# Retention in a six-stage Trainium2 kernel: rotation split by queries and keys, squares per head on ScalarE, layer norm on undivided numerators, and the output product in three one-pass products

## The reference

```
xn    = layernorm(x)
qkvg  = xn @ w_attn                       # 1024 q, 512 k, 512 v, 8 gates
log_g = log_sigmoid(6.906768 + gates)     # decay per token and key head
q, k  = rope(q), rope(k)
s     = q . k / 8
a     = exp(2*log(|s| + 1e-30) + cumsum(log_g)[t] - cumsum(log_g)[s] - max), 0 above the diagonal
num   = a @ v ;  den = sum(a)
y     = num / (den + 1e-6)
y     = (y - mean(y)) / sqrt(var(y) + 1e-9) * ln_w     # per head, 64 wide
x     = x + y @ w_proj                    # 1024 -> 512
```

## Time and profile before

| | |
|---|---|
| median of three runs | 2318.66 us |
| the profiled execution, its own time | 2317.28 us |
| its span, first to last instruction | 2315.5 us |
| TensorE busy | 2114.3 us, 91% |
| VectorE busy | 1419.9 us, 61% |
| ScalarE busy | 1362.7 us, 59% |
| GpSimd busy | 299.8 us, 13% |
| mean granted TensorE clock | 0.964 of full |
| retention stage | from 695 to 882 us of the span |

### The profile page before, as it was taken

How to read it: one execution, slowest core, us unless ns; L and a number is a source line. 1 busy time by engine, 2 the same in 40 slices (tenths; PEclk the granted TensorE clock), 3 DMA queues, 4 the chain that set the end, 5 groups by cost and what they waited for, 6 DMA issues and landing times. The chain is left out here.

```text
span 2315.5 us, 37828 instructions
## 1 busy us (share of the span) xinstructions
PE 2114.3 (91%) x14761; PEld 1633.6 (71%) x14761; DVE 1419.9 (61%) x2392; ACT 1362.7 (59%) x2595; POOL 299.8 (13%) x270
## 2 busy tenths in 40 slices
PE   6999999999968977799999979999999999866798
PEld 4777777777744545688888746877787777645676
DVE  5455555454544864499999854554554454667687
ACT  2566566566544433488888725666666665541675
POOL 2111112121110000100000221121111120101001
PEclk9999999999988988999999989999999999977999
DMA  4000010101004003599999730010100100022887
GB/s 155 19 23 35 20 38 20 38 19 38 1 1 179 1 1 130 223 386 367 356 358 364 268 141 19 20 38 19 38 20 19 38 20 19 2 73 105 325 336 265
DMA packets 53585, 262.34 MB, mean 113 GB/s; under 512 B 9496, under 2 KB 9880, under 8 KB 26528
## 3 DMA queue, kind: packets, MB, share of 16 engines
q1 hardware_dynamic: 47104, 244.71, 28.2%
q0 software_dynamic: 2560, 8.39, 1.1%
q10 hardware_dynamic: 3744, 6.82, 0.8%
HBM read 243.91 MB, written 15.99 MB: 112 GB/s over the span
## 5 line engine op out<-in xcount | busy, mean ns | idle before, releaser
L512 DVE COPY c_pt<-bank 128x512 f32<-128x512 f32 x256 | 177.0, 691 | 549.3 <-PE bank L341 549.2
L664 ACT ACTIVATE c_pr<-wide,c_nmax 128x512 f32<-128x512 f32 x512 | 349.3, 697 | 164.8 <-DVE c_nmax L504 83.8
L231 POOL TENSOR_TENSOR c_clo<-c_raw,c_chi 128x512 fp32r<-128x512 f32 x122 | 158.2, 1299 | 1012.1 <-ACT c_chi L641 1012.1
L341 PE MATMUL bank<-ident,c_pr 128*128 128x128 f32 x2048 | 268.7, 273 | 14.0 <-DVE c_pt L512 11.8
L341 PEld LDWEIGHTS bank<-ident,c_pr 128*128 128x128 f32 x2048 | 238.0, 140 | 49.9 <-DVE c_pt L512 14.0
L649 ACT ACTIVATE c_khi<-bank,c_cols 128x512 fp32r<-128x512 f32 x128 | 88.1, 688 | 252.2 <-PE bank L94 252.2
L92 PE MATMUL bank<-c_wv_hi,c_chi 128*128 128x512 f32 x512 | 218.2, 426 | 15.7 <-DVE c_clo L442 14.4
L1664 DVE TENSOR_TENSOR moe_wlo<-moe_raw,moe_whi 128x2048 fp32r<-128x2048 f32 x97 | 219.1, 2284 | 17.2 <-ACT moe_whi L1520 17.2
L92 PE MATMUL bank<-c_chi,c_wk_hi 128*128 128x512 f32 x512 | 213.7, 417 | 8.8 <-ACT c_v L655 8.7
L94 PE MATMUL bank<-c_wv_hi,c_clo 128*128 128x512 f32 x512 | 202.8, 396 | 0.0
L93 PE MATMUL bank<-c_wv_lo,c_chi 128*128 128x512 f32 x512 | 202.7, 396 | 0.0
(11 more groups left out here) (371 smaller groups left out, 4044.4 us busy)
## 6 DMA issues: line engine op xcount, KB each, us to landing
moe_hr<-in_L_ffn_w SPq DMA_DIRECT2D x68, 1024.0 KB, 7.0
moe_raw<-in_L_ffn_w SPq DMA_DIRECT2D x52, 1024.0 KB, 7.0
c_raw<-in_ctx SPq DMA_DIRECT2D x32, 1024.0 KB, 4.9
moe_raw<-in_L_ffn_we_gate SPq DMA_DIRECT2D x15, 1024.0 KB, 7.0
moe_raw<-in_L_ffn_we_up SPq DMA_DIRECT2D x15, 1024.0 KB, 6.6
moe_raw<-in_L_ffn_we_down SPq DMA_DIRECT2D x15, 1024.0 KB, 6.6
slot_outputs<-moe_ob ACTq DMA_DIRECT2D x26, 256.0 KB, 6.0
ret_w<-in_L_attn_w_attn SPq DMA_DIRECT2D x4, 1024.0 KB, 9.2
```

Source lines behind the costliest of these rows:

```text
L231: nc.gpsimd.tensor_tensor(clo[:, g % 2, c, :], raw[:, c, :], f32(chi[:, g % 2, c, :]), ALU.subtract) \
L341: last = pe.transpose(TB[n % 2][:, h * P:(h + 1) * P], pr[:, u % 2, h, n * P:(n + 1) * P], k["ident"][:])
L512: nc.vector.tensor_copy(pt[:, n, :], TB[0][:]).then_inc(pt_dve, 1)
L664: nc.scalar.activation(pr[:, u % 2, h, :], S[h][:], ACT.Exp, bias=nmax[:, b % 2, i, at:at + 1], scale=-1.0 if masked else 1.0, accum_out=d ...
```

## The change

- `rotate` is cut in two. `turn_pairs` makes the cosine and sine products for a range of heads. The 16 query heads are turned once projection groups 0 and 1 have been copied, ahead of the gate steps; the 8 key heads after them. `turn_qk` waits for the copies of all projection groups only from its second quarter on.
- `weigh` ends with the reciprocal; u is no longer multiplied. `squares` is 16 instructions, one for each head, each with that head's reciprocal as its scale, and releases `numerators` after every fourth.
- `divide` is gone. `standardise` takes sum, mean and deviations from the numerators in the banks, and the variance gets 1e-9 times the square of (den + 1e-6) instead of 1e-9.
- The product with ln_w leaves `scale`. ln_w is read as a column of 128 (two DMAs of 64 four-byte elements), and ScalarE scales w_proj with it while it makes its high part (`high_output`, 8 instructions, in block 0 ahead of the copy of projection group 0); VectorE makes the low part (`low_output`, 8 instructions, after the first `weigh`).
- The output product is made of three float32r products for each chunk, 24 in all. `keep_y` writes the high part of turned y, and VectorE the low part (`low_y`, two instructions, ahead of `standardise` of the next block), for which the products wait.

The core of the diff:

```diff
@@ TensorE, turn_qk
-                    pe.wait_ge(S["proj_read"], (b + 1) * NPJ)
-                    after(pe, S["y_copied"], 2 * (b - 1))
+                    after(pe, S["y_low"], 2 * (b - 1))
...
+                        if i == 1:
+                            pe.wait_ge(S["proj_read"], (b + 1) * NPJ)
@@ TensorE, numerators
-                    pe.wait_ge(S["squared"], b + 1)
                     for i in range(4):
+                        pe.wait_ge(S["squared"], 4 * b + i + 1)
@@ TensorE, output
-                    pe.wait_ge(S["wp_in"], 16)
+                    pe.wait_ge(S["wp_lo"], 2 * C)
                     for c in range(2 * C):
                         if c % 4 == 0:
-                            pe.wait_ge(S["y_copied"], 2 * b + c // 4 + 1)
-                        last = pe.matmul(ps[6][:], yT[:, c, :], wp[:, c, :], start=(c == 0), stop=(c == 2 * C - 1))
+                            pe.wait_ge(S["y_low"], 2 * b + c // 4 + 1)
+                        last = three_products(pe, ps[6][:], yT_hi[:, c, :], yT_lo[:, c, :], wp_hi[:, c, :], wp_lo[:, c, :],
+                                              c == 0, c == 2 * C - 1)
@@ ScalarE
                 def squares(b):
                     act.wait_ge(S["r_ready"], b + 1)
-                    nc.scalar.square(s_abs[:], u[:]).then_inc(S["squared"], 1)
+                    for h in range(QH):
+                        last = nc.scalar.activation(s_abs[:, h, :], u[:, h, :], ACT.Square, scale=ru[:, h:h + 1])
+                        if h % 4 == 3:
+                            last.then_inc(S["squared"], 1)
+
+                def high_output():
+                    act.wait_ge(S["wp_in"], 16)
+                    act.wait_ge(S["lnw_in"], 16 * (P // RD))
+                    for c in range(2 * C):
+                        nc.scalar.activation(wp_hi[:, c, :], wp[:, c, :], ACT.Identity, scale=lnw[:, 0:1]).then_inc(S["wp_hi"], 1)
...
                     magnitudes(b)
+                    if b == 0:
+                        high_output()
@@ VectorE, rotate
+                    dve.wait_ge(S["proj_read"], b * NPJ + 2)
+                    turn_pairs(slice(0, QH))
+                    s.wait()
+                    after(dve, S["qk_turned"], 4 * b)
+                    nc.vector.tensor_tensor(qr[:], qkr[:, 0:QH], qks[:, 0:QH], ALU.add).then_inc(S["rotated"], 1)
                     dve.wait_ge(S["proj_read"], b * NPJ + NPJ)
...
+                    turn_pairs(slice(QH, ROT))
@@ VectorE, weigh
-                    s.then(nc.vector.reciprocal(ru[:], um[:]))
-                    nc.vector.tensor_tensor(u[:], u[:], ru[:].unsqueeze(2).to_broadcast([P, QH, P]), ALU.mult) \
-                        .then_inc(S["r_ready"], 1)
+                    after(dve, S["squared"], 4 * b)
+                    nc.vector.reciprocal(ru[:], um[:]).then_inc(S["r_ready"], 1)
+                def low_y(b):
+                    for i in range(2):
+                        dve.wait_ge(S["y_copied"], 2 * b + i + 1)
+                        nc.vector.tensor_tensor(yT_lo[:, i * 4:(i + 1) * 4, :].rearrange("p c t -> p (c t)"), ps[4 + i][:],
+                                                f32(yT_hi[:, i * 4:(i + 1) * 4, :]).rearrange("p c t -> p (c t)"), ALU.subtract) \
+                            .then_inc(S["y_low"], 1)
@@ VectorE, standardise
                     for i in range(4):
                         dve.wait_ge(S["num"], 4 * b + i + 1)
+                        s.mark(nc.vector.reduce_sum(col[:, 0, four[i]], num[i][:, :, 0:RD], AX.X))
+                        s.mark(nc.vector.tensor_scalar_add(col[:, 1, four[i]], num[i][:, :, RD], 1e-6))
+                    s.wait()
+                    s.mark(nc.vector.tensor_scalar(col[:, 2, :], col[:, 0, :], 1.0 / RD, None, ALU.mult))
+                    s.then(nc.vector.scalar_tensor_tensor(out=col[:, 3, :], in0=col[:, 1, :], scalar=1e-9, in1=col[:, 1, :],
+                                                          op0=ALU.mult, op1=ALU.mult))
+                    for i in range(4):
+                        nc.vector.tensor_tensor(yc[:, four[i], :], num[i][:, :, 0:RD],
+                                                col[:, 2, four[i]].unsqueeze(2).to_broadcast([P, 4, RD]), ALU.subtract).then_inc(S["num_read"], 1)
@@ VectorE, order of the steps
                     weigh(b)
+                    if b == 0:
+                        low_output()
                     if b + 1 < NB:
                         rotate(b + 1)
-                    divide(b)
+                    if b > 0:
+                        low_y(b - 1)
                     standardise(b)
                     if b > 0:
                         add_output(b - 1)
                     scale(b)
+                low_y(NB - 1)
                 add_output(NB - 1)
```

76 lines of the change are left out of this document (38 added, 38 removed).

## The result

The changed kernel takes 2331.25 us (median of six executions, 2321.75 to 2333.87) against 2318.68 for the kernel before (six, 2317.19 to 2321.18). The ratio is 1.004, with a 95% interval from 1.0028 to 1.0052: slower, where 2312.6 was forecast. The profiled execution of the changed kernel took 2333.24 us (span 2331.5), 16.0 more than that of before.

A forecast was written before the change was run, and what follows sets the result against it. TensorE was taken to bound the middle of the retention stage, waiting for other engines in front and tail. Gains 0.6 + 0.1 + 1.1 + 0.45 + 3.75 = 6.0 us took the median 2318.66 to 2312.6, range 2308.5 to 2318.0.

The forecast's parts named there:

- Front: Retention stage up to block 0's scores: queries turned earlier, copies behind ScalarE's gates; 0.6 us gained, bounds 0 and 1.4.
- The squares: ScalarE, each block: 16 squares at 0.253 us, 4.05 us in all, making the v and gate copies late.
- E: Moment on TensorE when the transposes of the squares begin, 815.36 us in block 2; squares start 3.5 us before.
- rival A: ScalarE as bound: SBUF reads cost more, 0.288 us a head; gain 3.8 us, 2314.9; chance 0.19.
- The steady period: Block 2, between the scores of blocks 2 and 3: 37.1 us instead of 37.56, 0.45 gained.
- low-part wait: TensorE ahead of the output products: a new wait of 1.3 us for VectorE's first low half of y.
- The new wait on the weight copy in block 0: ScalarE's 4.8 us of weight casts precede projection group 0's copy; cover 0.35 us, beyond it every 0.1 costs 0.1.
- blocks 0 and 1: First two score periods of retention: cumulated gain 0.7 us through block 0 (0.1 its own), 1.1 in block 1.
- Tail: From block 3's scores to the stage's last addition: +43.0 us against 46.75, 3.75 gained.
- rival B: Tail: TensorE stays at half speed through the last products, 11 us; total gain 2.3, 2316.4; chance 0.11.
- C: Slower: squares do not overlap, 0.384 us each, 2321.0; decides from 0.347 a head; chance 0.08.
- D: Better: front gains 1.4 and the tail's clock rises at +37.5; gain 7.5 us, 2311.2; chance 0.09.

The follow-up runs named there:

- a2: Changed kernel plus nine unused transposes in each TensorE pause between the first and second quarter of the squares' transposes, all waits kept: 2320.42 us, ratio 0.9999.
- a3: Changed kernel with unused transposes in those pauses, plus 55 ahead of block 3's numerators and 18 ahead of its output: 2319.76 us, ratio 0.9994.
- a1: Changed kernel with u multiplied by the reciprocal on VectorE again and one square over all heads: 2313.74 us, ratio 0.9976.
- a5: Changed kernel with one float32 output product instead of three, squares per head kept: 2330.73 us, ratio 1.0037.
- b1: Kernel before with only the squares per head, reciprocal as scale, and the multiplication of u dropped: 2327.32 us, ratio 1.0037.
- b3: Kernel before with only the three one-pass output products, weights unscaled, low part of y ahead of the division: 2329.27 us, ratio 1.0041.
- b0_again: Kernel before, unedited, run once more: 2320.39 us, ratio 0.9997.
- a0_again: Changed kernel, unedited, run once more: 2328.45 us, ratio 1.0024.
- c4: Kernel before with queries turned first, LN undivided, ln_w in the weights, and block 2's output ahead of block 3's numerators: 2304.77 us, ratio 0.9938.
- b2: Kernel before with only the queries turned ahead of the keys: 2319.34 us, ratio 0.9991.
- c3: Kernel before with queries turned first, LN undivided and ln_w in the weights; one square, one float32 product: 2313.61 us, ratio 0.9964.
- c5: c4 plus 45 unused transposes between block 3's numerators and its y: 2307.95 us, ratio 0.9948.
- c1: Changed kernel with one square for all heads and block 2's output ahead of block 3's numerators: 2313.17 us, ratio 0.9957.
- c2: c1 plus 45 unused transposes ahead of the last output: 2309.57 us, ratio 0.9955.

## Why the prediction was wrong

**Front, -0.6 forecast, -0.53 measured.** Right in this profile and for its reason: queries are turned early and their copies stand behind the gates. It wasn't seen that the clock has a choice there, worth 2.8: the other outcome, 3.2 us gained (a2, 31.39), lies outside the bounds of 0 and 1.4 that the prediction gave.

**The squares, mis-sized.** The order of ScalarE's steps and the start of the squares (3.56 us ahead of E) came as forecast; the term is 0.293 and not 0.253 a head. 16 x 0.04 = 0.64, and the v copy starts at E + 1.13 where E + 0.49 was forecast. This was rival A, whose argument fits: the Silu row reads PSUM, the squares read SBUF. No run moved the source alone. By the Trainium skill, Perfetto Trace Analysis, section "Optimizing Scalar/DVE Operations", an instruction of ScalarE costs some 93 ns of access on SBUF and 51 on PSUM; the 42 between them agree with this case's 40. The 293 apart that follow from the figures of the Trainium skill, ScalarE: Activation LUTs, section "What ACT_TABLE_LOAD costs", and that the prediction set aside for the Silu row, are what the runs show. The row that was nearest by size and kind wasn't nearest by where it reads. The same 0.64 us also lengthens the pause: by the prediction's own times TensorE would have stood still for some 0.6 us between the first and second quarter (an estimate: the gate copy at 816.3, the quarter 0.31 behind it as in the rows of after, less the 0.64 that the first quarter takes from 815.36), and it stood for 1.26. Two small slips beside it change nothing: 1.15 less three times 0.253 is 0.391, not 0.384, and 622 less 590 gives 0.285 a head for rival A, not 0.288.

**The steady period, right.** Block 2 took 37.70 where 37.11 + 0.64 = 37.75 follow: low-part wait 1.54 (1.3), products 5.69 (834.63 to 840.32; 5.6), no wait on the addition ahead of the decay sum. The change was worth nothing there. The new wait on the weight copy in block 0 didn't come either: the copy of group 0 ended 10.0 us behind the scores, as forecast, and the projection ran through in 14.79 us.

**The step that failed: blocks 0 and 1 were costed at full clock.** The prediction had the second quarter of the transposes behind the late gates, and priced that as 0.7 us of lateness. It didn't ask what the idle time does to the clock: the clock was a question only in the front and the tail, behind pauses of 3.5 us and more. The fall behind 1.26 us cost 4.5 and 4.9 (a2_fill), 9.4 of the 15.7 us between forecast and measurement inside the stage; the tail is 4.8 of the rest and the dearer squares some 1.4. That these falls need the pause, and don't come from the later gate, is shown: a2 and a3 keep the gate late, fill the pause and have no fall, a1 removes the pause and has none, a5 keeps the pause and has both. What decides whether a given pause brings a fall isn't shown: the same 1.26 us had none in block 2, and b1's three had none.

**Tail, +43.0 forecast, +47.8 measured** (844.40 to 892.19). The reciprocal was ready at +10.6, as forecast, and LN of block 3 stood behind the low part of block 2's y, as forecast. But rival B's condition came, in another place: the clock stayed down for 27.3 us, from 849.8, through the transposes, the numerators (6.93 us, 3.25 more than at full clock and 2.61 more than in before) and half of block 2's products. In before it had been low for 13.6 us there. Why it stayed down twice as long is open: the transposes now come in two pieces, behind waits of 8.50 and 1.78 us, but in b1 they do so too (9.04 and 1.78) with 13.7 us, and b3, with one piece behind 12.00, has 23.9. The numerators ended at +24.7 where +21.5 was forecast. LN started at +27.7 where +24.05 was forecast. Block 2's products then ended so late that the residual addition (879.90) came 1.66 us after VectorE was free for it, ahead of block 3's scaling, and that put y at +37.6 (+32.6). Only the last products came as forecast: the clock fell once more at 883.9 and rose 3.1 us into them, and they took 7.3 us (7.0). The prediction had costed the second pause of the tail at half clock; for the first it let the clock rise as soon behind the pause as in before (4.9 us).

**Outside the stage, 6.3 us, costed at nothing.** 3.9 of them lie between the stage and the RWKV stage, where the code is the same. That stretch takes 1164.2 to 1164.5 us in before, b0_again, b1 and a5, and 1168 to 1170 in after, a0_again and most others, c4 among them. So it isn't tied to a slow or a quick retention. The window over the first 272 us behind retention shows TensorE at a clock of 0.95:

```profile
893.00:1165.00 272.00, 249.95 (x1191) 204.15 (x1192) 212.07 (x235) 196.41 (x260) 10.51 (x19) 0.95 0.80 307
```

The same stretch of before (883 to 1155) has 0.96. Windows of 1 us over the whole way to the RWKV stage tell the two lengths apart. In the four runs of 1164 us the clock is low five times, 51.2 us in all; in each of the fourteen others the first of these stretches is 17.1 us long instead of 13.7, and two more of 3.4 us come 448 to 450 and 1134 to 1136 us behind the first instruction of the next stage (in after the first of them begins at 1341.2: the granted clock from 1341 to 1344 is 0.55, where in before it is 1.00 from 1330 to 1334). That is 10.2 us more at the lower level in after; at half speed they cost 5.1 us at most, an estimate that fits the 3.9. So these 3.9 us go with the clock too. No run moved the later stages alone, so what brings these falls stays open. The longer stretch takes 4.8 us from c4 too (1169.0 for 1164.2), whose stage is 16.1 us shorter than before's while its profiled execution is only 10.2 faster.

**Rivals.** A right in size; B right in effect, its place another; C wrong (0.293 is below its 0.347) although its sign was right, so that a result on the slower side was luck for it; of D the front came also in a2, the whole gain only in kernels without the per-head squares. Of the signs of being wrong that the prediction named, one came: half clock beyond +39 of the tail (to +42.9). A rival "a pause of a microsecond in the middle lowers the clock" was missing.

## What to carry to other kernels

When a change puts a wait on TensorE in a stretch that was continuous, price its idle time twice: as lateness, and as a possible fall of the clock over all that follows until it rises; here 1.26 us of idle cost 4.5 and 4.9 where the clock fell, and nothing more than its lateness where it didn't. A finer split on a helper engine (16 squares for one) is paid per instruction and can move a pause into the critical engine's list even where the helper is far from full. And read a saving (three cheap products, 1.4 us) together with the operand it has to wait for, and with what else that operand's maker has in its queue: in b3 the low part made VectorE 1.2 us later a block, and that, not TensorE, set the block.

## What the hardware showed that was not expected

- The granted clock fell behind pauses of 1.26 us, among transposes and 65-column products, in a stretch that had been busy at full clock; and not behind the same pause in block 2 of the changed kernel or in the three blocks of b1. The Trainium skill, TensorE: Matmul & The Clock Gate, section "A second HAM failure mode: psum-queue depth-cycling", tells of another kernel, of 512-column bf16 matmuls, in which frequent short idles between groups of matmuls made the clock go down and up. The traces here agree that short idles can do it, and show it for single ones (falls in the changed kernel's blocks 0 and 1 and in b3's block 1, the lower level held for 3.4 to 13.7 us).
- With the queries turned first the front has two lengths, 31.3 to 31.5 us (a1, a2, b2, c3, c4, c5) and 33.8 to 34.2 (after, a0_again, a3, a5, c1, c2), with the same order of work there.
- The times of the changed kernel's executions go with their mean clock, though not strictly: 2321.75 us at 0.960 and 2325.37 at 0.959, but 2330.84 to 2333.87 at 0.954 to 0.956. So a median over few executions of such a kernel also measures how often the clock fell.
